# Turning W_v with VectorE and moving a tile's trip ahead of the last loads, in a cross-attention and feed-forward kernel

## The chip, the cores and the metric

The kernel runs on one core of a Trainium2 chip. The metric is the device time of one execution in microseconds (us). TensorE does matrix products and turns (transposes) into PSUM, VectorE and ScalarE do elementwise work, GpSimd a few small steps, and SyncE (SP) issues nearly all transfers from one queue, in order. Each engine runs its instructions in the order of the program and waits on semaphores.

## The reference

```python
x = x + attention(layernorm(x), ctx, Wq, Wk, Wv, Wout, bout)   # 8 heads of 128, 154 keys, softmax
y = layernorm(x)
y_prev = y shifted by one row, zeros in front
xr = mu_r * y + (1 - mu_r) * y_prev;  xk = mu_k * y + (1 - mu_k) * y_prev
r = sigmoid(xr @ W_r.T);  k = relu(xk @ W_k.T) ** 2
out = x + r * (k @ W_v.T)
```

x is (2, 2048, 512), the context (2, 77, 384), W_r, W_k and W_v are (512, 512), all float32. The context rows of both batches serve as 154 keys for every query.

## The kernel before, in words

The 4096 rows of x are 32 tiles of 128 rows. Keys and Wq are folded once into A (512 x 8 heads x 154), values and Wout into B, so a tile needs `scores` (x times A), a softmax over the keys of each head, and `attend` (probabilities times B). The feed-forward part works on pairs of tiles: `gate_rows` (r), `key_columns` (k) and `value_rows`. Every product is done in three passes: both operands are split into a high part, rounded to TensorE's fp32r, and a low part, the rest; high parts are written by ScalarE (`..._hi`), low parts by VectorE (`..._lo`).

Rows have to be turned before a product. The first two tiles of x are turned by TensorE. All others, the probabilities and the second norm's rows make a trip: the rows are stored to DRAM (`store_x`, `store_probs`, `store_x2`), fetched back in four quarters of 32 partitions (`hand_x`, `hand_probs`, `hand_x2`), and VectorE turns the 32 x 32 blocks (`x_turn`, `probs_turn`, `x2_turn`). W_k and W_r are loaded by quarters too (`load_quarters`) and turned by VectorE, four instructions each (`weights_turn`). W_v is loaded by plain rows (`load_rows`) and turned by TensorE in `turn_weights`, 16 turns into four PSUM banks (`W_BANKS`), from where ScalarE takes half of it as the high part and VectorE the low part.

The order of the work is written out by hand for each engine. Ahead of the loop over groups of four tiles (`turns(engine, step)`) stands a prologue that sets up A and B (`values_out`, `values_hi`, `values_lo`, `pack_values`) and works the first tiles in between. In that prologue:

- SyncE issues the loads, the fourth tile's x, `x_early[0]` (the fifth tile), W_v, eight small loads of mu, `x_early[1]`, and then the bias and the third tile's trip (`store_x(2)`, `hand_x(2)`).
- TensorE does the first and second tile's scores, `values_out` block by block (block 4 waits for the low part of block 0, for its bank), scores(2), attend(0), the turns of W_v, scores(3), attend(1), and then the loop, which starts with scores(4), attend(2).
- scores(t) waits for the tile's turned rows (`xT_ready`) and for the exponentials of the tile before, which read the same banks; scores(2) waits for all nine `B_lo`.
- `x_statistics(t)` on VectorE gives mean and variance, `x_root(t)` on GpSimd the factor and shift (three small instructions), `x_norm(t)` on ScalarE the normed rows.

The lines that order VectorE in the stretch that the change touches:

```python
            x_turn(2)
            maxima(1, 2)
            x_statistics(4, None, 1)
            for c in range(6):
                values_lo(c)
            x_lo(2)
            for c in range(6, FULL):
                values_lo(c)
            pack_values()
            probs_turn(0)
```

Of the kernel before, what the change touches and what calls it, by code (L numbers as in the profile page):

```python
# [11 lines left out]
P = 128  # L12
Q = 32
# [6 lines left out]
def xattn_ffn(nc, x, ctx_768, Wq, Wk, Wv, Wout, bout, W_r, W_k, W_v, mu_r, mu_k, out):  # L20
# [18 lines left out]
    HJ = HEADS * J  # L39

# [32 lines left out]
    with ExitStack() as stack:  # L73
# [51 lines left out]
        for w in "kr":  # L125
# [41 lines left out]
                 "v": sb("raw_wv", [P, DC, D], at=at_act)}  # L167
# [65 lines left out]
        Wv_turned, Wv_hi_ready, Wv_ready = sem("Wv_turned"), sem("Wv_hi_ready"), sem("Wv_ready")  # L233
# [91 lines left out]
        W_BANKS = [T[2], XB, T[0], T[1]]  # L325
# [5 lines left out]
        def _(sp):  # L331
# [18 lines left out]
            load_x_in(2)  # L350
            def load_quarters(w, src):
# [7 lines left out]
            sp.dma_start(x_early[0][:], xt[4 * P:5 * P, :]).then_inc(early_loaded[0], 16)  # L359
            load_rows(raw_w["v"], W_v, ffn_loaded["v"])  # L360
            with nc.allow_non_contiguous_dma(reason="two vectors of 512 as columns"):
                for w, src in (("k", mu_k), ("r", mu_r)):
                    for q in range(4):
                        part = src[q * P:(q + 1) * P].rearrange("(k i) -> i k", i=Q)
                        sp.dma_start(mu[w][q * Q:(q + 1) * Q, :], part).then_inc(mu_loaded, 16)  # L365

            sp.dma_start(x_early[1][:], xt[5 * P:6 * P, :]).then_inc(early_loaded[1], 16)

# [73 lines left out]
            def step(g, s):  # L442
# [21 lines left out]
            hand_x(2)  # L464
            sp.wait_ge(consts_ready, 1)
# [28 lines left out]
        def _(te):  # L494
# [64 lines left out]
            def gate_rows(q, j):  # L559
# [46 lines left out]

            def turn_weights(w):

                te.wait_ge(ffn_loaded[w], 16)
                te.wait_ge(exp_done, 6)  # L610
                te.wait_ge(B_ready, FULL)
                for c, bank in enumerate(W_BANKS):
                    for m in range(DC):
# [834 lines left out]
```

## Time and profile before

| what | value |
|---|---|
| median of three runs | 747.12 us (746.11 to 747.29) |
| the profiled execution | 747.18 us, span 745.4 us |
| granted TensorE clock | 1.000 |
| busy in the span | TensorE 737.6 us (99%), VectorE 514.5 (69%), ScalarE 426.1 (57%), GpSimd 123.7 (17%) |
| transfers | 106.52 MB, mean 143 GB/s |

Busy times are of one execution. Times in a timeline are us from the start of the span. A row gives the start, the duration, the engine, the line, what is written from what, and in brackets how long the engine was idle ahead of it and what ended that. Instructions that follow each other on one engine overlap a little, so the distance from start to start is shorter than the duration.

### The profile page before, as it was taken

The numbers are of one execution on the slowest core, as the hardware profiler recorded it, in microseconds if no ns is written. First come the engines' busy times: TensorE is split into PE (matmuls) and PEld (weight loads), VectorE is DVE, ScalarE is ACT, GpSimd is POOL, SyncE is SP. The second block draws the span as 40 slices with busy tenths as digits, with TensorE's granted clock in tenths as the row PEclk, the third lists the DMA queues.
The fourth block names the chain that finished last, engine by engine and source line by source line (L and its number), as shares of the span: only waits on it lengthen the run. The fifth ranks groups of instructions, "written<-read, shape, count | busy, mean of one in ns | idle before, by whom it ended". The sixth has DMA issues, their size and how long they took to land.

```text
span 745.4 us, 13579 instructions
## 1 busy us (share of the span) xinstructions
PE 737.6 (99%) x3964; PEld 643.7 (86%) x3964; DVE 514.5 (69%) x1081; ACT 426.1 (57%) x1204; POOL 123.7 (17%) x279
## 2 busy tenths in 40 slices
PE   9999999999999999999999999999999999999998
PEld 8958888898989888898888889888888988888887
DVE  3679797676777776667777666677666667776662
ACT  3559666564647547564655656465565646555332
POOL 1111010212121020212102021211202121120211
PEclk9999999999999999999999999999999999999999
DMA  8973644555444453544435354443535454343301
GB/s 331 264 203 106 188 115 145 148 150 162 141 132 146 137 158 99 176 134 146 139 120 162 95 176 136 150 133 123 159 105 166 140 163 128 113 155 93 110 29 43
DMA packets 85655, 106.52 MB, mean 143 GB/s; under 512 B 9951, under 2 KB 62073, under 8 KB 85627
## 3 DMA queue, kind: packets, MB, share of 16 engines
q1 hardware_dynamic: 85588, 106.15, 46.7%
q8 instruction: 13, 0.21, 0.1%
q14 instruction: 15, 0.12, 0.1%
q10 hardware_dynamic: 39, 0.04, 0.0%
HBM read 58.70 MB, written 47.45 MB: 142 GB/s over the span
## 4 chain that ended last, share of the span: by engine, by line
PE 86%; SPq 5%; DVE 4%; ACT 1%; issue 1%; DMA 1%; POOL 0%; DVEq 0%; POOLq 0%; ACTq 0%
PE ffn L497 12%; PE ffn L499 12%; PE ffn L498 12%; PE scores L498 8%; PE scores L499 8%; PE scores L497 8%; PE attended L498 8%; PE attended L499 8%; PE attended L497 8%; SPq L354 2%; SPq L338 1%; PE attended L547 1%; PE attended L546 1%; PE scores L653 1%; SPq L365 1%
## 5 line engine op out<-in xcount | busy, mean ns | idle before, releaser
L497 PE MATMUL scores<-A_hi,xT_hi 128*128 128x462 f32 x372 | 130.0, 349 | 1.1 <-DVE xT_lo L985 1.1
L498 PE MATMUL scores<-A_lo,xT_hi 128*128 128x462 f32 x372 | 130.3, 350 | 0.0
L499 PE MATMUL scores<-A_hi,xT_lo 128*128 128x462 f32 x372 | 129.9, 349 | 0.0
L499 PE MATMUL attended<-B_hi,pT_lo 128*128 128x512 f32 x288 | 112.4, 390 | 0.0
L498 PE MATMUL attended<-B_lo,pT_hi 128*128 128x512 f32 x288 | 112.3, 390 | 0.0
L497 PE MATMUL attended<-B_hi,pT_hi 128*128 128x512 f32 x288 | 112.1, 389 | 0.2 <-DVE pT_lo L985 0.2
L788 ACT ACTIVATE probs<-scores,neg_max 128x154 f32<-128x154 f32 x248 | 93.2, 388 | 33.2 <-DVE neg_max L1045 32.8
L1045 DVE TENSOR_REDUCE neg_max<-scores 128x3 f32<-128x462 f32 (+1 forms) x93 | 53.1, 583 | 70.8 <-PE scores L499 70.8
L1338 POOL TENSOR_SCALAR var<-stats 128x1 f32<-128x1 f32 x64 | 12.4, 194 | 461.8 <-DVE stats L991 460.8
L497 PEld LDWEIGHTS scores<-A_hi,xT_hi 128*128 128x128 f32 x372 | 70.1, 189 | 8.6 <-DVE xT_lo L985 1.6
L498 PEld LDWEIGHTS scores<-A_lo,xT_hi 128*128 128x128 f32 x372 | 70.0, 188 | 5.6
L499 PEld LDWEIGHTS scores<-A_hi,xT_lo 128*128 128x128 f32 x372 | 69.9, 188 | 5.2
L985 DVE TENSOR_TENSOR pT_lo<-pT,pT_hi 128x512 fp32r<-128x512 f32 (+1 forms) x96 | 47.9, 554 | 38.3 <-ACT pT_hi L814 38.2
L497 PE MATMUL ffn<-xk_hi,WkT_hi 128*128 128x256 f32 x256 | 72.6, 283 | 0.1
L499 PE MATMUL ffn<-xk_hi,WkT_lo 128*128 128x256 f32 x256 | 72.4, 283 | 0.0
L498 PE MATMUL ffn<-xk_lo,WkT_hi 128*128 128x256 f32 x256 | 72.4, 283 | 0.0
L762 ACT ACTIVATE normed<-x_in,shift,rstd 128x512 f32<-128x512 f32 x30 | 24.5, 815 | 71.0 <-POOL shift L1343 70.5
L797 ACT ACTIVATE probs<-probs,inv_sum 128x154 f32<-128x154 f32 x192 | 63.9, 426 | 0.6 <-DVE inv_sum L1056 0.4
L499 PEld LDWEIGHTS attended<-B_hi,pT_lo 128*128 128x128 f32 x288 | 54.1, 188 | 11.3
L497 PEld LDWEIGHTS attended<-B_hi,pT_hi 128*128 128x128 f32 x288 | 54.1, 188 | 10.7 <-issue 0.4
L498 PEld LDWEIGHTS attended<-B_lo,pT_hi 128*128 128x128 f32 x288 | 54.0, 188 | 10.4
L1005 DVE STREAM_TRANSPOSE pT<-probs_handed 128x1408 f32<-128x1408 f32 x32 | 52.6, 1644 | 0.1
(176 smaller groups left out, 1549.2 us busy)
## 6 DMA issues: line engine op xcount, KB each, us to landing
prob_rows<-probs SPq DMA_DIRECT2D x32, 704.0 KB, 3.4
probs_handed<-prob_rows SPq DMA_DIRECT2D x128, 176.0 KB, 3.3
x_rows<-normed SPq DMA_DIRECT2D x61, 256.0 KB, 2.1
handed<-x_rows SPq DMA_DIRECT2D x244, 64.0 KB, 1.9
x_in<-in_x SPq DMA_DIRECT2D x32, 256.0 KB, 3.6
out<-x SPq DMA_DIRECT2D x31, 256.0 KB, 2.3
wq<-in_L_xattn_Wq SPq DMA_DIRECT2D x2, 1024.0 KB, 10.4
wout<-in_L_xattn_Wout SPq DMA_DIRECT2D x1, 2048.0 KB, 19.5
```

Of the source, the lines that this page charges most:

```text
L338: sp.dma_start(x_in[i][:], xt[i * P:(i + 1) * P, :]).then_inc(x_loaded[i], 16)
L354: sp.dma_start(raw_w[w][q * Q:(q + 1) * Q, :, :], rows[q]).then_inc(ffn_loaded[w], 16)
L497: te.matmul(psum, left[0], right[0], start=first, stop=False)
L498: te.matmul(psum, left[0], right[1], start=False, stop=False)
L499: return te.matmul(psum, left[1], right[0], start=False, stop=last)
L762: nc.scalar.activation(to, rows, ACT.Identity, bias=shift1[:], scale=rstd1[:]).then_inc(xn_ready, 1)
L788: last = nc.scalar.activation(probs[:, q, cols], score_banks(t)[b][:, (h - h0) * J:(h - h0 + 1) * J], ACT.Exp, bias=neg_max[:, h:h + 1], a ...
L797: last = nc.scalar.mul(probs[:, q, cols], probs[:, q, cols], inv_sum[:, h:h + 1])
L985: return v.tensor_tensor(dst, value, hi.bitcast(F32), ALU.subtract)
L1005: return v.transpose(dst.rearrange("p k (r i) -> p r k i", i=Q), src.rearrange(blocks, r=4, k=width, i=Q))
L1045: v.tensor_reduce(neg_max[:, h0:h1], score_banks(t)[b][:, 0:(h1 - h0) * J].rearrange("p (h j) -> p h j", j=J), X, ALU.max, negate=True).th ...
L1338: gp.tensor_scalar(var[:], stats[:, 1:2], EPS, 1.0, ALU.add, ALU.mult).then_inc(var_ready, 1)
```

## The change

1. W_v is loaded by quarters like W_k and W_r, and VectorE turns it (four instructions). TensorE's 16 turns are gone, and with them their wait and the banks. ScalarE's high part and VectorE's low part of W_v read the turned copy in SBUF; the copy lies where the low part will be.
2. W_k's turned rows come in another order, which fits the order of the values that the turned W_v expects.
3. SyncE issues the bias and the third tile's trip right behind the fourth tile's load. `x_early[0]`, W_v, the mu loads and `x_early[1]` follow it, ahead of `store_probs(0)`.
4. VectorE does `values_lo` 0 to 3 ahead of `x_turn(2)`; the turns of W_v stand between the last `values_lo` and behind them; `x_statistics(4)` comes behind the low parts of the first probabilities. `weights_lo("v")` comes behind `maxima(3, ...)`, `x_turn(4)` and `x_lo(4)` ahead of other steps, and `add_x(1)` ahead of `pack_lo(3)`.
5. In the loop, `load_x` stands ahead of `store_probs` on SyncE, `x_statistics` ahead of `open_values` on VectorE, and `x_root` ahead of `output` on GpSimd.

```diff
@@ allocations @@
-            if w != "v":
-                turned_w[w] = sb(f"W{w}T", [P, DC, D], at=at_low)
+            turned_w[w] = sb(f"W{w}T", [P, DC, D], at=at_low)
...
-                 "v": sb("raw_wv", [P, DC, D], at=at_act)}
+                 "v": sb("raw_wv", [P, 4 * DC, P], at=at_act)}
@@ sync @@
             load_quarters("r", W_r)
             load_x_in(3)
-            sp.dma_start(x_early[0][:], xt[4 * P:5 * P, :]).then_inc(early_loaded[0], 16)
-            load_rows(raw_w["v"], W_v, ffn_loaded["v"])
-            ...
-            sp.dma_start(x_early[1][:], xt[5 * P:6 * P, :]).then_inc(early_loaded[1], 16)
...
+                if is_tile(t + 4) and is_tile(t):
+                    load_x(t + 4, s)
                 if is_tile(t + 2):
                     store_probs(t + 2)
-                if is_tile(t + 4) and is_tile(t):
-                    load_x(t + 4, s)
...
             load_bias()
             store_x(2)
             hand_x(2)
+            sp.dma_start(x_early[0][:], xt[4 * P:5 * P, :]).then_inc(early_loaded[0], 16)
+            load_quarters("v", W_v)
+            ...
+            sp.dma_start(x_early[1][:], xt[5 * P:6 * P, :]).then_inc(early_loaded[1], 16)
             sp.wait_ge(consts_ready, 1)
             store_probs(0)
@@ tensor @@
-                    te.wait_ge(W_ready, 2 * DC)
-                    te.wait_ge(Wv_ready, DC)
+                    te.wait_ge(W_ready, 3 * DC)
...
             attend(0)
-            turn_weights("v")
             scores(3)
@@ scalar @@
             def weights_hi(w):
                 for c in range(DC):
+                    act_e.wait_ge(W_turned, DC * "krv".index(w) + DC)
                     if w == "v":
-                        act_e.wait_ge(Wv_turned, c + 1)
-                        nc.scalar.mul(WT[w][0][:, c, :], W_BANKS[c][:], 0.5).then_inc(Wv_hi_ready, 1)
+                        nc.scalar.mul(WT[w][0][:, c, :], turned_w[w][:, c, :], 0.5).then_inc(W_hi_ready, 1)
@@ vector @@
                 dve.wait_ge(ffn_loaded[w], 64)
-                to = turned_w[w][:].rearrange("p k (b r i) -> p b r k i", r=4, i=Q)
+                if w == "v":
+                    dve.wait_ge(W_turned, 2 * DC)
+                order = "p k (r b i) -> p b r k i" if w == "k" else "p k (b r i) -> p b r k i"
+                to = turned_w[w][:].rearrange(order, r=4, i=Q)
...
+                if comes_in_steps(t + 3):
+                    x_statistics(t + 3, (s + 3) % 4, g + (s + 3) // 4 + 1)
                 if half == 0 and is_pair(q - 1) and not is_last(t - 1):
                     open_values(q - 1, 1)
-                if comes_in_steps(t + 3):
-                    x_statistics(t + 3, (s + 3) % 4, g + (s + 3) // 4 + 1)
...
             maxima(1, 1)
+            maxima(1, 2)
+            for c in range(4):
+                values_lo(c)
             x_turn(2)
-            maxima(1, 2)
-            x_statistics(4, None, 1)
-            for c in range(6):
+            for c in range(4, 6):
                 values_lo(c)
             x_lo(2)
+            weights_turn("v", range(0, 1))
             for c in range(6, FULL):
                 values_lo(c)
+                weights_turn("v", range(c - 5, c - 4))
             pack_values()
...
             for i in range(3):
                 probs_lo(0, i)
+            x_statistics(4, None, 1)
...
-            weights_lo("v")
             for b in range(3):
                 maxima(3, b)
+            weights_lo("v")
+            x_turn(4)
             inverse_early(3)
-            x_turn(4)
+            x_lo(4)
             normalise_late(3)
-            x_lo(4)
+            add_x(1, 0, 1)
             pack_lo(3)
-            add_x(1, 0, 1)
@@ gpsimd @@
+                if comes_in_steps(t + 3):
+                    x_root(t + 3)
                 if half == 0 and is_pair(q - 1):
                     output(q - 1, 1, (s + 1) % 4)
-                if comes_in_steps(t + 3):
-                    x_root(t + 3)
```

## Rows read from the trace of the kernel before

**Rows 1.** Windows view, 180 to 700 us: busy us of each engine, granted clock.

```profile
180.00:700.00 520.00, 520.00 (x2714) 457.06 (x2713) 361.99 (x770) 300.18 (x863) 90.53 (x192) 1.00 0.45 139
```

**Rows 2.** Timeline of TensorE, prologue: start, us, line, what, idle before.

```profile
48.13 1.04 PE L653 MATMUL spare<-wout,vT 128*32 128x512 f32 x8
50.45 1.06 PE L653 MATMUL scores<-wout,picked 128*32 128x512 f32 x8 [1.28 <-DVE B_lo L985]
...
57.46 0.48 PE L497 MATMUL scores<-A_hi,xT_hi 128*128 128x462 f32 x1
...
70.88 0.60 PE L614 MATMUL ffn<-identity,raw_wv 128*128 128x128 f32 x4
...
72.55 0.46 PE L497 MATMUL scores<-A_hi,xT_hi 128*128 128x462 f32 x1
...
79.36 0.39 PE L497 MATMUL attended<-B_hi,pT_hi 128*128 128x512 f32 x1
...
87.27 0.48 PE L497 MATMUL scores<-A_hi,xT_hi 128*128 128x462 f32 x1 [1.15 <-DVE xT_lo L985]
```

**Rows 3.** Waits of TensorE: who for whom, us in total, times, longest.

```profile
PE attended L497 <- DVE pT_lo L985: 0.2, 1, 0.2
```

**Rows 4.** Timeline of VectorE, prologue.

```profile
39.11 0.69 DVE L988 BATCH_NORM_STATS2 raw<-x_in 128x6 f32<-128x512 f32 x1 [1.26 <-DMA x_in<-in_x]
...
44.42 1.30 DVE L1145 STREAM_TRANSPOSE WrT<-raw_wr 128x512 f32<-128x512 f32 x2
...
47.86 0.72 DVE L1005 STREAM_TRANSPOSE xT<-handed 128x512 f32<-128x512 f32 x1 [1.63 <-DMA handed<-x_rows]
...
49.64 0.18 DVE L991 BATCH_NORM_AGGREGATE stats<-raw 128x2 f32<-128x6 f32 x1
...
53.92 0.69 DVE L985 TENSOR_TENSOR B_lo<-scores,B_hi 128x512 fp32r<-128x512 f32 x1 [0.17 <-ACT B_hi L860]
...
56.50 0.69 DVE L985 TENSOR_TENSOR B_lo<-scores,B_hi 128x512 fp32r<-128x512 f32 x1
57.66 0.69 DVE L1166 TENSOR_TENSOR packed_rows<-scores,bias_rows 128x512 f32<-128x512 f32 x1 [0.48 <-PE scores L653]
...
62.56 1.49 DVE L985 TENSOR_TENSOR pT_lo<-pT,pT_hi 128x512 fp32r<-128x512 f32 x3
...
78.11 1.50 DVE L985 TENSOR_TENSOR pT_lo<-pT,pT_hi 128x512 fp32r<-128x512 f32 x3 [0.69 <-ACT pT_hi L814]
...
81.95 1.56 DVE L1045 TENSOR_REDUCE neg_max<-scores 128x3 f32<-128x462 f32 x3
...
86.52 0.69 DVE L985 TENSOR_TENSOR xT_lo<-xT,xT_hi 128x512 fp32r<-128x512 f32 x1
```

**Rows 5.** Timeline of ScalarE, prologue.

```profile
64.56 0.81 ACT L762 ACTIVATE normed<-x_early,shift,rstd 128x512 f32<-128x512 f32 x1
...
71.06 0.38 ACT L788 ACTIVATE probs<-scores,neg_max 128x154 f32<-128x154 f32 x1
```

**Rows 6.** Timeline of GpSimd: last of x_root's three instructions, fifth and sixth tile.

```profile
51.01 0.27 POOL L1343 TENSOR_SCALAR shift<-stats,rstd 128x1 f32<-128x1 f32 x1 [0.18 <-POOL rstd L1340]
...
67.75 1.28 POOL L1343 TENSOR_SCALAR shift<-stats,rstd 128x1 f32<-128x1 f32 x1 [0.18 <-POOL rstd L1340]
```

**Rows 7.** Timeline of SyncE's queue: start and duration of the issues.

```profile
16.46 7.38 SPq L354 DMA_DIRECT2D raw_wk<-in_L_ffn_W_k  x4
...
33.33 3.50 SPq L365 DMA_DIRECT2D mu_k_cols<-in_L_ffn_mu_k  x4
...
46.43 0.36 SPq L397 DMA_DIRECT2D prob_rows<-probs  x1
...
49.61 1.91 SPq L406 DMA_DIRECT2D probs_handed<-prob_rows  x4
```

**Rows 8.** DMA view, 24 to 30 us, while W_k and W_r load.

```profile
DMA packets 2130, 1.18 MB, mean 197 GB/s; under 512 B 73, under 2 KB 2047, under 8 KB 2130
```

**Rows 9.** Tile probs_handed, 49 to 60 us.

```profile
DMA to landing us min/median/max: 2.7/3.5/4.4
```

More of the change, by code:

```diff
@@ L358, in _ @@
             load_x_in(3)
-            sp.dma_start(x_early[0][:], xt[4 * P:5 * P, :]).then_inc(early_loaded[0], 16)
-            load_rows(raw_w["v"], W_v, ffn_loaded["v"])
[L361 to L365, printed above, removed]
-            sp.dma_start(x_early[1][:], xt[5 * P:6 * P, :]).then_inc(early_loaded[1], 16)
             def load_bias():
@@ L464, in _ @@
             hand_x(2)
+            sp.dma_start(x_early[0][:], xt[4 * P:5 * P, :]).then_inc(early_loaded[0], 16)
+            load_quarters("v", W_v)
+            with nc.allow_non_contiguous_dma(reason="two vectors of 512 as columns"):
+                for w, src in (("k", mu_k), ("r", mu_r)):
+                    for q in range(4):
+                        part = src[q * P:(q + 1) * P].rearrange("(k i) -> i k", i=Q)
+                        sp.dma_start(mu[w][q * Q:(q + 1) * Q, :], part).then_inc(mu_loaded, 16)
+            sp.dma_start(x_early[1][:], xt[5 * P:6 * P, :]).then_inc(early_loaded[1], 16)
             sp.wait_ge(consts_ready, 1)
@@ L605, in last_value_rows @@
                     last.then_inc(last_done, 1)
[L607 to L613, printed above, removed]
-                        last = te.transpose(bank[:, m * P:(m + 1) * P], raw_w[w][:, m, c * P:(c + 1) * P], identity[:])
-                    last.then_inc(Wv_turned, 1)
             def step(g, s):
@@ L848, in weights_hi @@
                 for c in range(DC):
+                    act_e.wait_ge(W_turned, DC * "krv".index(w) + DC)
                     if w == "v":
-                        act_e.wait_ge(Wv_turned, c + 1)
-                        nc.scalar.mul(WT[w][0][:, c, :], W_BANKS[c][:], 0.5).then_inc(Wv_hi_ready, 1)
+                        nc.scalar.mul(WT[w][0][:, c, :], turned_w[w][:, c, :], 0.5).then_inc(W_hi_ready, 1)
                     else:
-                        act_e.wait_ge(W_turned, DC * "kr".index(w) + DC)
                         copy(WT[w][0][:, c, :], turned_w[w][:, c, :]).then_inc(W_hi_ready, 1)
@@ L1149, in weights_lo @@
                     hi, lo = WT[w][0][:, c, :], WT[w][1][:, c, :]
+                    dve.wait_ge(W_hi_ready, DC * "krv".index(w) + c + 1)
                     if w == "v":
-                        dve.wait_ge(Wv_hi_ready, c + 1)
-                        v.scalar_tensor_tensor(out=lo, in0=W_BANKS[c][:], scalar=0.5, in1=hi.bitcast(F32),
-                                               op0=ALU.mult, op1=ALU.subtract).then_inc(Wv_ready, 1)
+                        v.scalar_tensor_tensor(out=lo, in0=turned_w[w][:, c, :], scalar=0.5, in1=hi.bitcast(F32),
+                                               op0=ALU.mult, op1=ALU.subtract).then_inc(W_ready, 1)
                     else:
-                        dve.wait_ge(W_hi_ready, DC * "kr".index(w) + c + 1)
                         low_part(lo, turned_w[w][:, c, :], hi).then_inc(W_ready, 1)
```

2 lines of the change are left out of this document (removed).

## Prediction

> **What bounds the kernel now.** I read the busy times by stretch first: from 180 to 700 us TensorE computes 520.00 of 520 us, with VectorE and ScalarE well below [rows 1]; what little it idles lies ahead of 100 us or at the very end. So only three things can move the end: TensorE work taken away or added, gaps closed or opened in the prologue, and a stage that becomes slower than TensorE. The edits inside the loop cannot pay: there is no gap there to close. The list of waits of TensorE and its timeline then give what the prologue has to give: one gap in front of the fifth values block, where block 3 starts at 48.13 and block 4 at 50.45. Block 4 (twice the work) to block 10 take from 50.45 to the scores at 57.46, so a single one about 0.86, and block 4 could start at 48.99: 1.46 us. The turns of W_v run from 70.88 to 72.55: 1.67 us of work. The last gap is in front of the fifth tile's scores: they start at 87.27, while attention that starts at 79.36 and lasts 6.60 ends at 85.96: 1.31 us [rows 2]. A small one of 0.2 us follows ahead of the third tile's attention [rows 3]. All together 4.6 us, 0.6% of the time: that is the most the change can bring.
>
> **The removed gap at the values.** It was made by VectorE: it waited 1.63 us for the third tile's trip, turned it at 47.86, and only behind that came the first B_lo (statistics of the fifth tile, whose second half is at 49.64, stood between too) [rows 4]. The new order does B_lo 0 to 3 first, and the trip's turn behind them, so block 4 starts at 48.99. From there the B_hi parts come 1.46 us earlier. But VectorE now has other work in that stretch: one turn of W_v ahead of each of B_lo 6, 7, 8, at 0.61 us from start to start (two in a row took 1.30 with their overlap, the row at 44.42). B_lo 5 starts at 53.92 - 1.46 = 52.46; x_lo 53.06; turn 53.66; B_lo 6 54.27; turn 54.87; B_lo 7 55.48; turn 56.09; B_lo 8 at 56.70, against 56.50 before [rows 4]. The third tile's scores wait for all nine: 56.70 + 0.69 = 57.39, against a start at 57.46 [rows 2]. **Term 1: 0.0 us.** The gap of 1.46 moves from block 4 to just ahead of these scores. The fourth turn stands ahead of pack_values: 57.91 instead of 57.66, and so does all that VectorE does behind it: +0.25.
>
> **The removed turns on TensorE.** The fourth tile's scores could start at 70.9 instead of 72.55. They need bank 0 free, that is the third exponential of the third tile: the fourth one starts at 71.06 [rows 5], so 71.1 is the floor even with nothing late. But ScalarE will be late. Its queue has the fifth tile's x_norm ahead of W_k's and W_r's high parts and of those exponentials. It ran at 64.56 without a wait, because the statistics were from 49.64 [rows 4, 5]. Now x_statistics(4) stands behind the low parts of the first tile's probabilities. These start at 62.56 + 0.25 = 62.81 and take 1.41; the statistics start at 64.22, the aggregate at 65.02. From aggregate to x_norm there are GpSimd's three instructions: aggregate at 49.64, third one from 51.01 to 51.28, so 1.64 and a hop of 0.04: x_norm at 66.70, **2.14 us late** [rows 4, 6]. The other bound of that trip: the same third instruction took 1.28 instead of 0.27 when it ran beside W_k's low parts (67.75) [rows 6], so up to 1.0 more; I take the short one, since maxima (which read one operand in PSUM) will run beside it. ScalarE has no slack to lose in this stretch: the casts, the exponentials and the normalisation follow back to back. So bank 0 comes free at 71.1 + 2.14 = 73.3 and the scores start there, 0.8 later than before, though TensorE was ready at 70.9.
>
> The same 2.14 travel on: normalise, pack_hi, pack_lo, the turn of the second tile's probabilities, and their first low part at 78.11 + 2.14 = 80.25 [rows 4], complete at 80.8. Scores end at 73.4 + 6.8 = 80.2, so attention starts at 80.85 against 79.36 [rows 2] and ends at 87.5. From 80.25 VectorE does what stood from 78.11 to 81.95 (three low parts of the probabilities and four of W_v, 3.84), three maxima (1.56, less the overlap 1.46) and the turn of the fifth tile (0.64 to the next start) [rows 4]: 86.2; ScalarE's exponentials of the fourth tile end at 86.3 and its x_hi at 86.9; x_lo ends at 87.6. Before, x_lo started at 86.52 and ended at 87.2 [rows 4]. Here the lateness is mostly absorbed, for the old order had ScalarE wait for the maxima behind W_v. **Term 2: the fifth tile's scores start at 87.7 instead of 87.27: +0.43.** The 1.67 us of turns have become waiting for ScalarE.
>
> **The moved loads.** SyncE's queue is in order. The third tile's store and trip come ahead of x_early, W_v, eight mu parts and x_early. The last tile load ahead of it lands at 39.1 (VectorE waits for it until 39.11 [rows 4]); the store lands right behind, about 40.1. Then four issues of the trip 1.9, x_early 0.4, W_v's four, the mu parts, x_early 0.4, and only then store_probs(0), which was issued at 46.43 [rows 7]. Four issues cost 1.9 with an empty queue (49.61) and 7.4 behind a full one (16.46). The queue is empty here: I take 1.9. Four mu parts took 3.50, so eight 3.8 to 7.0; I take 5.4 [rows 7]. That gives 50.1 for store_probs(0), 3.7 late. It landed 3.2 after its issue (46.43 to 49.61). W_v now comes in pieces of 512 bytes like W_r: 2130 packets in 6 us [rows 8], so 2048 take 5.8 us, from 42.5 to 48.3, and the mu parts are behind them: I put the landing at 54.0 against 49.6. Trip issued over 1.9, landing 2.7 to 4.4 behind the last issue [rows 9]: complete 58.2 to 59.9, I take 59.4. VectorE wants it at 57.91 + 0.80 = 58.71. **Term 3: 0.7 us** (0 to 1.2 by these rows). It moves the whole chain of term 2 one for one. By a fit of the Trainium skill (DMA: Bandwidth & Descriptors, Anatomy of one DMA, made for GpSimd's path) a transfer takes about 2.0 us and its bytes at 436 GB/s, whatever the size of its pieces; that would be an estimated 4.4 us for W_v's megabyte, it would be through before the mu parts are issued, and the sum would be 747.2. The row, 197 GB/s with pieces of 512 bytes, speaks against it [rows 8]. W_v itself is needed at 53.66 and landed about 50, so its new wait costs nothing; were it late, B_lo 6 to 8 and the third tile's scores stand behind it.
>
> **What costs nothing.** W_v's low parts now read SBUF instead of PSUM: the tensor_tensor of both kinds goes at 0.60 from start to start. W_k's turned row order changes an output stride only. add_x(1) ahead of pack_lo(3) starts 1 us earlier the trip to the second tile's x2_norm, on which the third attention waited: the 0.2 gap and its restart (0.3) go: **term 4: -0.3**. In the loop, statistics ahead of open_values, load_x ahead of store_probs and x_root ahead of output move waits of engines that TensorE does not wait for [rows 1]. If that cover were gone, load_x would cost store_probs about 0.9 us (wait for x2 and an issue) per tile.
>
> **Sum.** 0.0 + 0.43 + 0.7 - 0.3 = +0.8 us on a span of 745.4, whose execution took 747.18; the median of the runs is 747.12. Forecast 747.9.
>
> **The rivals.**
> A, faster: ScalarE's lateness doesn't arise, because x_statistics(4) or its GpSimd trip finds a place earlier, or ScalarE's chain has slack that the rows don't show. Then only the +0.25 of VectorE's queue is left. Scores at 71.4, attention at 79.0 (its low parts at 78.36 + 0.55), x_lo(4): 78.36 + 3.84 + 1.46 + 0.64 = 84.3, ScalarE's x_hi and x_lo 1.3: 85.6. That is 1.6 earlier, and with term 4 745.2. With no chain of VectorE in the way the limit is 747.1 - 4.6 = 742.5. For it: TensorE really loses 1.67 us of work. Against: [rows 5, 6], in which nothing hides the trip through GpSimd.
> B, slower: the probabilities' trip is what decides. W_v's issues go at the speed of W_k's: 7.4 instead of 1.9, and store_probs(0) follows at 55.6, it is through at 58.8, and the trip lands about 63.8, 5.1 behind 58.71: 752.3. It decides from the point where the trip lands over 60.1 (1.4 behind 58.71), which is +1.5. For it: these are the same strided quarters. Against: W_k was issued behind all the attention's weights, W_v behind nothing. In between lies 749 to 750, with a loaded queue or the slow GpSimd trip (+1.0).
> C: the probabilities arrive in time; term 3 is 0, 747.2. It is also what the Trainium skill's fit above would give.
>
> **How the numbers follow.** Forecast 0.42 (747.2 to 748.6), C 0.16, A 0.15, B and what lies between 0.27. A measurement of this kernel tells about 0.2%, 1.5 us, from no change. C and the forecast are within it: same 0.58; A faster 0.15; B slower 0.27. The likeliest case's own range is 747.0 to 748.7; with A's first figure and the lower half of B the range is 745.2 to 750.0.
>
> **What the profile after would show.** TensorE's waits: none ahead of block 4, a new one of 1 to 1.5 us ahead of the third tile's scores at 57.4 (from B_lo), one of about 2 ahead of the fourth tile's (from the exponentials, near 73), a short one at 80, and the fifth tile's scores at 87.7 or later. ScalarE: an idle of about 2 us ahead of x_norm(4), ended by GpSimd's shift. VectorE: a wait for the probabilities at 58.7 that is term 3. The prediction is wrong if x_norm(4) runs near 65, or if store_probs(0) is issued near 48 or near 55.

## The result, and the profile after

| | kernel before | kernel after |
|---|---|---|
| median, 19 runs each | 747.21 us (745.94 to 749.98) | 747.90 us (746.79 to 749.16) |
| ratio to before | | 1.0013 [1.0007, 1.0019] |
| profiled execution | 747.18 us, span 745.4 | 747.85 us, span 746.1 |

The time went up by 0.13%, which is inside the 0.2% that the prediction held for "no change". A later comparison of the kernel before with itself gave 1.0011 [1.0002, 1.0020], so a tenth of a per cent is at the limit of what can be told here. The forecast was 747.9. As will be seen, part of that agreement is luck: the sum held one term that didn't arise, and lacked two effects that did.

The busy times on the page after (busy us, share of the span, instructions):

```profile
PE 737.1 (99%) x3948; PEld 644.1 (86%) x3948; DVE 516.5 (69%) x1085; ACT 428.2 (57%) x1204; POOL 123.6 (17%) x279
```

The longest of TensorE's waits after (us in total, times, longest):

```profile
PE scores L494 <- ACT probs L773: 2.3, 1, 2.3
PE scores L494 <- DVE B_lo L969: 1.4, 1, 1.4
PE ffn L650 <- DVE normed L1208: 1.0, 1, 1.0
PE attended L494 <- DVE pT_lo L969: 0.4, 1, 0.4
```

The window of [rows 1] in the kernel after:

```profile
180.00:700.00 520.00, 520.00 (x2714) 457.11 (x2714) 361.77 (x771) 300.81 (x859) 88.89 (x188) 1.00 0.45 139
```

The loop is as full as before. (The 1.0 on `normed` is in the first two us of the span, in both kernels.) Two waits stand in the prologue where there were none: 1.4 us for the last B_lo and 2.3 us for the exponentials. This is where they are in TensorE's timeline, with the start of the first tile's scores ahead of them:

```profile
33.34 0.45 PE L494 MATMUL scores<-A_hi,xT_hi 128*128 128x462 f32 x1
...
58.89 0.45 PE L494 MATMUL scores<-A_hi,xT_hi 128*128 128x462 f32 x1 [1.41 <-DVE B_lo L969]
...
74.75 0.45 PE L494 MATMUL scores<-A_hi,xT_hi 128*128 128x462 f32 x1 [2.29 <-ACT probs L773]
...
82.15 0.47 PE L494 MATMUL attended<-B_hi,pT_hi 128*128 128x512 f32 x1 [0.41 <-DVE pT_lo L969]
```

And the same start before:

```profile
31.92 0.45 PE L497 MATMUL scores<-A_hi,xT_hi 128*128 128x462 f32 x1
```

Here is the first thing to see. Ahead of these scores both programs issue the same matmuls, and yet one profile comes to them at 31.92 and the other at 33.34. Over all 14 profiles of this study it is 31.3 to 33.8. (What sets it is told in the last section.) So a profile after can't be laid on one of before by the clock on the wall. From here on TensorE's steps are counted from the start of the first scores, and "less 1.42" turns a time of the profile after into one of before. The steps, from the timelines (us from the first scores; the last column is from the first key_columns to the end of the span):

| kernel | first scores at | third tile's scores | fourth's | second attention | fifth's scores | third attention | key_columns | to the end | from first scores to the end |
|---|---|---|---|---|---|---|---|---|---|
| before | 31.92 | 25.54 | 40.63 | 47.44 | 55.35 | 62.48 | 71.88 | 641.60 | 713.48 |
| before, again | 32.51 | 25.32 | 40.42 | 47.24 | 55.13 | 62.27 | 71.69 | 641.40 | 713.09 |
| after | 33.34 | 25.55 | 41.41 | 48.81 | 55.46 | 62.23 | 71.54 | 641.22 | 712.76 |
| after, again | 33.41 | 25.55 | 41.41 | 48.80 | 55.51 | 62.27 | 71.58 | 641.21 | 712.79 |

Read by row, the change is 0.8 to 1.0 late at the fourth tile's scores, 0.1 to 0.4 late at the fifth's, level or up to 0.3 ahead at the third attention, and from the first key_columns to the end it takes 0.2 to 0.4 less. From the first scores to the end it is 0.3 to 0.7 us **shorter** than before, though its time is 0.7 longer. That is what the experiments have to explain, besides the two waits.

The instructions on which terms 2 and 3 rested, VectorE first:

```profile
55.09 0.70 DVE L1132 STREAM_TRANSPOSE WvT<-raw_wv 128x512 f32<-128x512 f32 x1
...
58.09 0.65 DVE L969 TENSOR_TENSOR B_lo<-scores,B_hi 128x512 fp32r<-128x512 f32 x1
58.67 0.69 DVE L1132 STREAM_TRANSPOSE WvT<-raw_wv 128x512 f32<-128x512 f32 x1
...
60.04 1.65 DVE L989 STREAM_TRANSPOSE pT<-probs_handed 128x1408 f32<-128x1408 f32 x1
...
66.34 0.18 DVE L975 BATCH_NORM_AGGREGATE stats<-raw 128x2 f32<-128x6 f32 x1
...
81.31 1.50 DVE L969 TENSOR_TENSOR pT_lo<-pT,pT_hi 128x512 fp32r<-128x512 f32 x3 [0.69 <-ACT pT_hi L799]
```

GpSimd's last step for the fifth tile's x_norm:

```profile
67.70 0.27 POOL L1333 TENSOR_SCALAR shift<-stats,rstd 128x1 f32<-128x1 f32 x1 [0.18 <-POOL rstd L1330]
```

and the x_norm itself on ScalarE:

```profile
68.00 0.82 ACT L747 ACTIVATE normed<-x_early,shift,rstd 128x512 f32<-128x512 f32 x1 [1.76 <-POOL shift L1333]
```

SyncE's queue (start and duration of the issues):

```profile
40.86 2.47 SPq L353 DMA_DIRECT2D raw_wv<-in_L_ffn_W_v  x4
43.37 2.67 SPq L460 DMA_DIRECT2D mu_k_cols<-in_L_ffn_mu_k  x4
46.08 1.86 SPq L460 DMA_DIRECT2D mu_r_cols<-in_L_ffn_mu_r  x4
47.99 0.43 SPq L461 DMA_DIRECT2D x_early<-in_x  x1
48.53 0.36 SPq L386 DMA_DIRECT2D prob_rows<-probs  x1
...
52.68 2.40 SPq L395 DMA_DIRECT2D probs_handed<-prob_rows  x4
```

No idle time stands in front of the turns of W_v or of the turn of the probabilities: both had landed. ScalarE waited 1.76 us for GpSimd's shift, as a chain of one statistics, one trip through GpSimd and one x_norm.

### The profile page after: what moved, and what is told of

Read it like the earlier page. It is cut to its first block, busy times and chain, and to the rows that moved or that the text cites. A ratio compares the mean times of both kernels' runs of the same rounds, so it can differ in the third digit from the quotient of the medians.

```text
span 746.1 us, 13557 instructions
## 1 busy us (share of the span) xinstructions
PE 737.1 (99%) x3948; PEld 644.1 (86%) x3948; DVE 516.5 (69%) x1085; ACT 428.2 (57%) x1204; POOL 123.6 (17%) x279
## 3 DMA queue, kind: packets, MB, share of 16 engines
HBM read 58.70 MB, written 47.45 MB: 142 GB/s over the span
## 4 chain that ended last, share of the span: by engine, by line
PE 93%; DVE 3%; ACT 2%; issue 1%; POOL 0%; POOLq 0%; DVEq 0%; ACTq 0%
PE ffn L494 12%; PE ffn L496 12%; PE ffn L495 12%; PE scores L495 9%; PE scores L496 9%; PE scores L494 9%; PE attended L496 8%; PE attended L495 8%; PE attended L494 8%; PE attended L544 1%; PE attended L543 1%; PE scores L670 1%; PE scores L639 1%; PE scores L701 1%; PE ffn L701 1%
## 5 line engine op out<-in xcount | busy, mean ns | idle before, releaser
L830 ACT ACTIVATE gate<-ffn 128x512 f32<-128x512 f32 x32 | 19.2, 598 | 64.0 <-PE ffn L496 64.0
```

The costliest lines, as they stand in the source:

```text
L830: nc.scalar.activation(gate[half][:], T[0][:], ACT.Tanh, scale=0.5).then_inc(gate_ready, 1)
```

## The experiments

The theory to be tested was the prediction's: the turns' time on TensorE has become two waits, one for VectorE's B_lo and one for ScalarE behind a late x_norm, and the probabilities' trip decides a further 0.7. Its rivals were those of the prediction: that ScalarE's lateness costs nothing (A's side), and that the moved loads and the trip behind them decide (B's side). All ratios are to the kernel before, run beside each.

**after_again.** The changed kernel, unchanged, beside the first three edits.

> The changed kernel once more, unchanged. In the profiles so far TensorE's first scores start at 31.92 us (before) and 33.34 us (after), though nothing ahead of them is changed, while from there to the end the changed kernel is 0.7 us shorter. If that head is chance, it will differ from run to run and the first scores start anywhere from 31.9 to 33.5 or later; from them to the end the profile again takes 712.8 us. If the head belongs to the changed program, the first scores start at 33.3 again. Ratio to the kernel before: 1.000 to 1.002.

Measured: 749.0 us, ratio 1.0026 [1.0015, 1.0037], 8 runs; 712.79 from the first scores. All steps fall on those of the first profile to 0.05 us. The median is 1.1 above that of the first comparison, though the work is the same: see the clock, below.

**stats_early.** The fifth tile's statistics back to where they had been relative to the maxima; all else as after.

```diff
             maxima(1, 2)
+            x_statistics(4, None, 1)
             for c in range(4):
...
                 probs_lo(0, i)
-            x_statistics(4, None, 1)
```

> The changed kernel with the fifth tile's statistics in VectorE's idle time ahead of the first B_lo, where its load has landed. Theory (ScalarE waits for x_norm(4) and hands the wait on to the fourth tile's scores): no wait of ScalarE ahead of x_norm(4), the wait of TensorE for the exponentials ahead of the fourth tile's scores falls from 2.3 to about 0.5 us, from first scores to end 1.8 us shorter than the changed kernel (711.0), ratio to before about 0.9985. Rival (the time is lost to VectorE's added turns and the quartered load of W_v): the wait moves elsewhere and the span stays within 0.4 us of the changed kernel's.

Measured: 746.21 us, 0.9982 [0.9973, 0.9992]; 711.13 from the first scores, 1.6 less than after. TensorE's waits:

```profile
PE scores L494 <- DVE B_lo L969: 1.4, 1, 1.4
...
PE attended L494 <- DVE pT_lo L969: 0.7, 1, 0.7
PE scores L494 <- ACT probs L773: 0.4, 1, 0.4
```

The wait for the exponentials fell from 2.3 to 0.4, and nothing ahead of it moved. So the moved statistics were the cause of it, through GpSimd and ScalarE's queue: term 2's chain is shown.

**turns_late.** W_v's turns out from between the B_lo, one by one into later places; W_r's second low parts make room.

```diff
             x_lo(2)
-            weights_turn("v", range(0, 1))
             for c in range(6, FULL):
                 values_lo(c)
-                weights_turn("v", range(c - 5, c - 4))
...
             add_x(0, 0, 0)
+            weights_turn("v", range(0, 1))
...
-            weights_lo("r", range(2, 4))
+            weights_turn("v", range(1, 3))
             pack_lo(2)
             probs_turn(1)
+            weights_turn("v", range(3, 4))
...
             inverse_early(3)
+            weights_lo("r", range(2, 4))
```

> The changed kernel with W_v's four turns taken from between the last B_lo and put into later idle times of VectorE (two low parts of W_r move behind for them). Theory: the wait of 1.4 us for B_lo ahead of the third tile's scores is gone, they start 25.5 us behind... that is 24.1 us instead of 25.55 us behind the first scores; VectorE and ScalarE are about 2 us earlier from there, x_norm(4) still waits for GpSimd; first scores to end 1.4 to 2.0 us shorter than the changed kernel. Rival: the trip of the first probabilities, now behind W_v's load, lands too late for the earlier turn, VectorE waits for it and less than 0.8 us is won.

Measured: 747.18 us, 1.0004 [0.9993, 1.0015]; 711.95 from the first scores. The third tile's scores came at 24.07 instead of 25.55 and the wait for B_lo was gone, so term 1 is shown: the three turns took up the 1.46 us of the gap that the new order had closed. The fourth tile's scores were still 1.6 earlier than in after (39.79 against 41.41). But only 0.8 of 1.5 was left at the end. TensorE's timeline tells why:

```profile
73.34 0.45 PE L494 MATMUL scores<-A_hi,xT_hi 128*128 128x462 f32 x1 [2.12 <-ACT probs L773]
73.62 0.37 PE L495 MATMUL scores<-A_lo,xT_hi 128*128 128x462 f32 x1
73.83 0.37 PE L496 MATMUL scores<-A_hi,xT_lo 128*128 128x462 f32 x1
...
75.57 0.59 PE L496 MATMUL scores<-A_hi,xT_lo 128*128 128x462 f32 x1
75.95 0.59 PE L494 MATMUL scores<-A_hi,xT_hi 128*128 128x462 f32 x1
...
77.88 0.40 PE L496 MATMUL scores<-A_hi,xT_lo 128*128 128x462 f32 x1
78.12 0.38 PE L494 MATMUL scores<-A_hi,xT_hi 128*128 128x462 f32 x1
```

The windows of the same stretch (busy time and count of TensorE, its weight loads, VectorE, ScalarE, GpSimd, then the granted clock, the DMA share and GB/s):

```profile
73.30:74.40 1.10, 1.06 (x5) 1.02 (x6) 1.00 (x3) 1.10 (x7) 0.17 (x1) 1.00 1.14 224
74.40:77.90 3.50, 3.50 (x12) 3.00 (x11) 2.73 (x8) 3.47 (x13) 0.86 (x3) 0.51 0.27 50
```

The like stretch in the profile of after_again:

```profile
74.80:78.00 3.20, 3.18 (x15) 2.91 (x16) 2.24 (x7) 3.20 (x16) 1.57 (x3) 1.00 0.66 140
```

Behind an idle of 2.12 us TensorE took up work at 0.21 us from start to start, and from 74.45 to 77.88 it went at 0.38: the granted clock of that window is 0.51, the lower level of 1.2 GHz. It did there nine matmuls in the time of some sixteen: about 1.5 us lost, of which 1.0 is seen at the second attention. It came 8.36 behind the fourth tile's scores instead of 7.40 in after, where some 0.6 had gone into waiting anyway (without a wait it is 6.8, as in before). The Trainium skill (TensorE: Matmul & The Clock Gate, Back-to-back issue gap) gives, for a matmul by itself, the columns divided by the clock from start to start, and 2.5 ns more at the upper level. By that 462 columns at 1.2 GHz are an estimated 0.385 us, and the trace agrees (0.384 on the mean of seven); at 2.4 GHz they would be 0.195, where the trace has 0.21. In after_again's profile the clock stayed whole behind the same wait.

**both.** The two edits together.

> Both edits. If the two waits stand in one chain, the gains add: about 3 us from first scores to end against the changed kernel, ratio to before 0.996 to 0.997. If ScalarE, busy without a gap from 60 to 80 us, is the limit, the second edit adds less than half of what it brings alone.

Measured: 745.9 us, 0.9986 [0.9974, 0.9997]; but 712.93 from the first scores, no less than after, where 3 us less was expected. The first scores began at 31.27 in this profile, the earliest of all, and VectorE waited for the probabilities' trip:

```profile
58.70 1.65 DVE L989 STREAM_TRANSPOSE pT<-probs_handed 128x1408 f32<-128x1408 f32 x1 [2.47 <-DMA probs_handed<-prob_rows]
```

TensorE's waits in it:

```profile
PE attended L494 <- DVE pT_lo L969: 2.6, 2, 1.4
PE scores L494 <- ACT probs L773: 1.1, 1, 1.1
```

The trip landed at 58.7 here and by about 58.6 in the profile after, though TensorE began 2 us earlier here. With VectorE's queue 2.4 shorter and TensorE 2 us early, that is late. So in this order the wait of term 3 exists, and it depends on when the first scores begin.

**both_probs_first.** both, with the mu loads and x_early[1] behind the probabilities' trip.

```diff
-            [mu loads, x_early[1]]
             sp.wait_ge(consts_ready, 1)
             store_probs(0)
             store_x(3)
             hand_probs(0)
             hand_x(3)
+            [mu loads, x_early[1]]
```

> The variant with both edits, and SyncE does the whole trip of the first probabilities and of the fourth tile ahead of the mu loads and x_early 1. In the profile with both edits VectorE waited 2.5 us for that trip, which landed at 58.7. Theory: the trip lands before VectorE wants it (about 56), the third tile's attention follows its scores, and from first scores to end the two gains add at last: 709.8 to 710.6 us, ratio to before 0.9955 to 0.997. Rival: ScalarE, which has no idle time from 60 to 80 us, is the limit, and it stays at 711.1 like the early statistics alone.

Measured: 745.52 us, 0.9972 [0.9960, 0.9984]; 710.63 from the first scores, which began at 33.77. hand_probs(0) was issued at 50.27 instead of 53.41, and VectorE turned the probabilities at 58.85 without a wait. A new wait of 1.3 us for pT_lo came ahead of the second attention, where the moved turns of W_v now stand. As the head differed by 2.5 us between this profile and that of both, the 2.3 us between them are not the edit's alone.

**mu_late and stats_early_mu_late.** The same loads behind store_probs(0) and store_x(3) only, in after and in stats_early.

```diff
+            sp.wait_ge(consts_ready, 1)
+            store_probs(0)
+            store_x(3)
             [mu loads, x_early[1]]
-            sp.wait_ge(consts_ready, 1)
-            store_probs(0)
-            store_x(3)
```

> The changed kernel with the eight loads of mu and x_early 1 issued behind the store of the first probabilities and of the fourth tile, in the time in which SyncE waits for the store to land. store_probs(0) is issued 5 us earlier (about 44 instead of 48.5), but its trip waits for the issues of mu, so hand_probs(0) starts at 50 to 51 instead of 52.7. If the moved loads cost the changed kernel time through the first probabilities' trip when TensorE's head is early (term 3 of the prediction), the median falls by 0.3 to 0.9 us. If VectorE's turns alone set the turn of these probabilities, nothing changes: 0.0 +- 0.2.

> The variant with early statistics, and the mu loads late. ScalarE's wait is gone and the trip is earlier: with an early head the whole gain of 1.65 us shows from first scores to end (711.1) and the median is 0.3 to 0.9 us below that of the early statistics alone; if the trip never matters, the same as with early statistics alone, ratio to before 0.998.

Measured: 747.53 us, 1.0006 [0.9997, 1.0015], and 712.76 from the first scores, with the same steps and waits as after to 0.03 us; 745.88 us, 0.9983 [0.9974, 0.9992], and 711.17 against 711.13. In the profiles of after's order the probabilities' trip is not on the path, and term 3 is zero. (No profile of after itself has an early head, so for those executions this rests on the medians, which hardly differ.) The second also repeats stats_early with a head of 31.73 in place of 33.27, and its profiled span is 742.9 against 744.4: in these kernels a late head goes through to the end, one for one.

**old_loads.** After, with x_early[0], W_v's quarters, the mu loads and x_early[1] ahead of the bias and the trip, where the kernel before has them.

> The changed kernel with the loads in their old order: x_early 0, W_v by quarters, mu and x_early 1 ahead of the third tile's trip. It shows what the moved trip is worth once W_v comes in pieces of 512 bytes. The queue is loaded there, so W_v's four issues should take 5 to 7 us and the third tile's store be issued at 44 to 48; its turn on VectorE, now behind four B_lo, waits 1 to 6 us, and the third tile's scores and all behind them are 1 to 5 us late: 714 to 718 us from first scores to end. If the issues go at 0.5 us each, it is within 0.5 us of the changed kernel's 712.8.

Measured: 747.72 us, 1.0008 [0.9999, 1.0018]; 714.45 from the first scores, 1.7 more than after. W_v's four issues took 3.85 us, less than expected. SyncE's queue:

```profile
37.23 4.97 SPq L364 DMA_DIRECT2D mu_k_cols<-in_L_ffn_mu_k  x4
42.25 2.07 SPq L364 DMA_DIRECT2D mu_r_cols<-in_L_ffn_mu_r  x4
...
45.67 0.38 SPq L375 DMA_DIRECT2D x_rows<-normed  x1
...
48.19 1.75 SPq L380 DMA_DIRECT2D handed<-x_rows  x4
```

hand_x(2) goes at 48.19 instead of 38.59, TensorE waits 0.6 us for B_lo at a values block, and the third tile's scores are 0.8 later (26.35). The fourth tile's scores are 0.8 later too (42.22 against 41.41), but the second attention is 1.8 later (50.58 against 48.81). Between them lies a fall of the clock like that of turns_late; its window, from about 1 us behind the wait for the exponentials:

```profile
75.70:79.20 3.50, 3.50 (x11) 3.01 (x10) 2.47 (x7) 3.47 (x13) 1.42 (x3) 0.51 0.29 57
```

So with W_v in quarters the moved trip is worth 0.8 us by the steps, and the other 0.9 of this profile are the clock's. The medians don't show even the 0.8: old_loads is at 1.0008, after at 1.0013 and 1.0026.

**trip_first_only.** The kernel before, with the trip ahead of the loads and VectorE's maxima, statistics and four values_lo ahead of the trip's turn. W_v stays in plain rows on TensorE, the loop stays.

```diff
+            [bias, store_x(2), hand_x(2)]
             [x_early[0], load_rows W_v, mu loads, x_early[1]]
-            [bias, store_x(2), hand_x(2)]
...
-            x_turn(2)
             maxima(1, 2)
             x_statistics(4, None, 1)
-            for c in range(6):
+            for c in range(4):
+                values_lo(c)
+            x_turn(2)
+            for c in range(4, 6):
                 values_lo(c)
```

> The kernel before with only the third tile's trip ahead of the loads, B_lo 0 to 3 ahead of its turn, and the statistics of the fifth tile ahead of those; W_v is loaded by rows and turned by TensorE as before. Theory: the gap of 1.46 us at values block 4 closes and nothing fills it, the third tile's scores start 24.1 us behind the first instead of 25.54, VectorE's chain is earlier by as much, and from first scores to end it takes 1.0 to 1.5 us less than before (712.0 to 712.5), as good as or better than the full change (712.8). Rival: what the full change gains comes from the turns taken off TensorE, then this one gives less than 0.5 us.

Measured: 746.50 us, 0.9990 [0.9981, 0.9999]; 711.92 from the first scores. The third tile's scores came at 24.07: the gap ahead of block 4 was closed with one part of the change, and this part alone ends 0.8 to 0.9 earlier than the whole.

**loop_only.** The kernel before, with the three edits of the loop.

> The kernel before with only the three edits inside the loop (load_x ahead of store_probs, statistics ahead of open_values, x_root ahead of output). The prediction costs them at nothing: the first 100 us are as before, and from the first key_columns to the end it takes 641.2 to 641.6 us as before. If one of them delays a step that TensorE needs, the stretch is longer by 0.1 us or more per tile, 3 us or more.

Measured: 746.50 us, 0.9990 [0.9980, 0.9999]; from the first key_columns to the end 641.25 against 641.60 and 641.40. But it also had no gap ahead of block 4, which lies ahead of the loop and which nothing in it could have closed: the third tile's scores came at 24.08. Its head was 33.80. VectorE's row for the trip's turn:

```profile
47.74 0.71 DVE L1005 STREAM_TRANSPOSE xT<-handed 128x512 f32<-128x512 f32 x1 [0.65 <-DMA handed<-x_rows]
```

TensorE's rows of blocks 3 and 4:

```profile
50.04 1.04 PE L653 MATMUL spare<-wout,vT 128*32 128x512 f32 x8
50.90 1.04 PE L653 MATMUL scores<-wout,picked 128*32 128x512 f32 x8
```

The trip landed at 47.7 as before (47.86 in [rows 4]), but TensorE was 1.9 us later, so there was nothing left to wait for. In the kernel before, then, the gap takes up what the head loses: its profiled spans are 745.4, 745.6 and (with the loop's edits) 745.5 for heads of 31.92, 32.51 and 33.80.

**base_again.** The kernel before, unchanged: see the table above.

> The kernel before once more, unchanged. The profiles of the changed kernel and of two variants had their first scores at 33.3 to 33.6 us, those of the kernel before and of the variant with both edits at 31.9 and 31.3. If the head is chance in every program, this profile may show either, and from first scores to end it takes 713.5 us. If the changed programs have the later head by themselves, this one shows 31.9 or earlier again. Ratio to the kernel before 1.000.

Measured: 747.34 us, 1.0011 [1.0002, 1.0020]; 713.09 from the first scores.

**pe_turns_full.** trip_first_only with the loop's edits and the new order of VectorE at the fourth tile: all of the change but for W_v's turns, which stay on TensorE, and the statistics, which stay ahead of values_lo. It differs from stats_early in who turns W_v, how it is loaded, where its low parts come from, and the order of W_k's turned rows.

```diff
+            [the three edits of the loop]
-            weights_lo("v")
             for b in range(3):
                 maxima(3, b)
+            weights_lo("v")
+            x_turn(4)
             inverse_early(3)
-            x_turn(4)
+            x_lo(4)
             normalise_late(3)
-            x_lo(4)
+            add_x(1, 0, 1)
             pack_lo(3)
-            add_x(1, 0, 1)
```

> The variant with early statistics, all its orders kept, but W_v loaded by rows and turned by TensorE as before. It isolates the turns. If taking 1.67 us of turns off TensorE is worth something by itself, this one is slower than the early statistics (711.1 us from first scores to end), by up to 1.7 us. If VectorE's four added turns give it back, both take the same within 0.3 us, since without them the third tile's scores start 1.46 us earlier.

Measured: **743.58 us, 0.9952 [0.9939, 0.9966]**, the fastest of the study, 3.6 us below the kernel before, in five runs. From the first scores to the end it took 709.82, 1.3 less than stats_early. (The two ratios, 0.9952 and 0.9982, lie some 2.2 us apart; the steps account for 1.3 of it. The rest may be the heads of the runs, which only a profile shows.) All of TensorE's waits:

```profile
PE ffn L663 <- DVE normed L1221: 1.0, 1, 1.0
PE scores L592 <- ACT normed L771: 0.3, 1, 0.3
PE ffn L697 <- DMA wq<-in_L_xattn_Wq: 0.3, 1, 0.3
```

All three lie ahead of the first scores or at the end of the span. Its turns of W_v, with the fourth tile's scores right behind:

```profile
69.50 0.60 PE L613 MATMUL ffn<-identity,raw_wv 128*128 128x128 f32 x4
69.93 0.60 PE L613 MATMUL spare<-identity,raw_wv 128*128 128x128 f32 x4
70.37 1.04 PE L613 MATMUL ffn<-identity,raw_wv 128*128 128x128 f32 x8
71.16 0.46 PE L496 MATMUL scores<-A_hi,xT_hi 128*128 128x462 f32 x1
```

The 1.66 us of turns are paid, and the view shows no wait of TensorE between the first scores and 718 us.

## Why the prediction came out as it did

**What bounds the kernel.** Right. The loop is full in every profile, and all that moved lay in the prologue, but for 0.2 to 0.4 us. Of the 4.6 us that the gaps and turns had to give, pe_turns_full took 3.3 to 3.7 (709.82 against 713.09 and 713.48): the gaps, without the turns, and the loop's part.

**Term 1, 0.0.** Right, to 0.01 us: 25.55 against 25.54, and the gap of 1.41 in front of these scores instead of block 4. B_lo 8 at 58.09 less 1.42 is 56.67; forecast 56.70. turns_late shows that the three turns are the cause.

**Term 2, +0.43.** The mechanism is right, step by step: x_norm(4) at 66.58 (forecast 66.70), the fourth tile's scores at 73.33 (73.4), the second attention at 80.73 (80.85), all less 1.42. The short value for GpSimd's third instruction was the right one (0.27). The size at the fifth tile's scores was off: 0.11 instead of 0.43 (0.3 against the kernel before's second profile). The step that failed there is "the same 2.14 travel on ... their first low part at 78.11 + 2.14 = 80.25": it came at 81.31 less 1.42, 79.89, and the 0.36 are what is missing at the end. x_norm itself was 2.02 late, and 0.24 more were made up on ScalarE, where the normalisation starts right behind the last exponential; in the kernel before it started 0.27 later than that. stats_early shows the cause of the lateness and what it is worth: 1.65.

**Term 3, +0.7.** This failed: it was 0. The prediction named store_probs(0) near 48 as a sign against it, and it was issued at 48.53, not 50.1. The step that failed first is the start of the third tile's trip. The prediction let its store land at 40.1, behind the last tile load of the queue; hand_x(2), which waits for that store, was issued at 38.59, and this 1.5 is nearly all of the 1.6. Behind it W_v's issues took 2.47 (1.9 taken) and the mu loads 4.53 (5.4 taken), together 0.3 less. The store of the probabilities was through by 52.68 at the latest (54.0 taken), and the pieces of the trip landed 2.6 to 3.5 us behind their issues, so by about 58.6 (59.4 taken); both shows 58.70. VectorE wanted them at 60.04. Less 1.42 that is 58.62, near the forecast's 58.71. So with a head as early as before's the two would just have met: the measured 0 is the lower of the term's bounds (0 to 1.2). The sum set a landing that goes by the wall's clock against a wish that moves with TensorE's head. mu_late settles that nothing hangs on it at a head of 32.94; for the earliest heads it stays open whether a few tenths do. The Trainium skill's fit (DMA: Bandwidth & Descriptors, Anatomy of one DMA), which made this rival C, doesn't hold for W_v: for a quarter of 262144 bytes it gives an estimated 2.6 us, and the rows have 4.7 to 6.7 from issue to landing. The trip was in time without it.

**Term 4, -0.3.** Right: from the fifth tile's scores to the third attention 6.77 instead of 7.13, and no wait there.

**The loop, 0.** A little off: from the first key_columns to the end the eleven profiles with the loop's edits take 641.2 to 641.3, the three without 641.4 to 641.6. That is 0.1 to 0.4 us less; the medians can't tell it from nothing, and what brings it was not looked for.

**What the sum left out.** By its steps the change should have ended 0.3 to 0.7 earlier, and its time was 0.7 later. Two effects lie between. Each is shown in profiles; how much each weighs in the medians is argued, since a run without a profile doesn't show its head:

- **The head.** In the kernel before the gap ahead of block 4 is a wait for a trip that lands near 47.8 on the wall's clock, so it absorbs a late head (loop_only). The new order ends that dependence, and then a late head costs all that it is late: 745.7, 746.1 and 746.2 for heads of 32.94, 33.34 and 33.41 (mu_late and the two of after). The prediction took a gap of 1.46 as something that can be won; in executions with a late head it isn't there.
- **The clock.** 12 of the 19 runs of after had a mean granted clock of 1.000 and a median of 747.74 us; the other 7 had 0.998 or 0.995, and a median of 749.06. That is 1.3 us more; turns_late's profile shows 1.5 of TensorE's time lost in one stretch behind the wait, 1.0 of it at the next step. Over the kernels whose longest wait in the prologue is 2.1 to 2.3 us (after, after_again, mu_late, old_loads, turns_late) 29 of 60 runs were at 0.998 or below. Over stats_early, stats_early_mu_late, trip_first_only, both_probs_first, loop_only and pe_turns_full, where it is 1.4 or less, none of 56 was; nor was any of the 87 runs of the kernel before beside them. It isn't the wait alone: mu_late had 1 of 11 with the same wait, and base_again 1 of 11 and both 2 of 12 without it. Two profiles have the fall, turns_late and old_loads, both about 1 us behind that wait. That it is at the same place in after's own runs is argued, since both profiles of after have the clock whole. Its price in the medians isn't settled either: between the runs with and without the lower mean clock it is 0.7 in turns_late (10 and 2 runs) and 0.1 in old_loads (5 and 5), where the head, unknown in them, may hide it.

So the wait of term 2 was priced at its length; in a part of the executions a fall of the clock comes with it, and in the two profiles that have it that cost about 1.0 more at the next step.

**The rivals.** A, the faster one, needed the statistics at an earlier place; stats_early is just that, at 746.2 (A said 745.2). B did not arise: W_v's issues went at 2.47, near the lower bound. C is what the trace shows (the trip in time); its 747.2 lacked the two effects above, as the forecast did. That the forecast's 747.9 fell on the median is in part luck: errors of opposite sign.

**Where the gain of the turns went.** 1.67 us of work left the engine that bounds the kernel, and 2.4 us came onto VectorE, just where VectorE's chain sets when scores(2) may start. pe_turns_full against stats_early says it in one number: by the steps, leaving the turns on TensorE is 1.3 us better. In both_probs_first, where the turns stood later, the chain of the second tile's probabilities took their place as the limit. TensorE came to the fourth tile's scores 1.26 earlier than in pe_turns_full (37.92 against 39.18), and yet the second attention started 0.2 later (46.17 against 46.00), behind a wait of 1.3. VectorE's first low part for it began at 45.33 there and at 44.74 in pe_turns_full. Attention started 0.84 behind that in both_probs_first, so an estimate from these rows is that with no turn at all in VectorE's way it could start at 45.6, 0.4 earlier than with the turns on TensorE. By that estimate most of the 1.67 us of turns lay in time that TensorE would have waited. It isn't settled whether a place for them exists where they would cost nothing.

## What to carry to other kernels

Work taken off the engine that is busy 99% of the time pays only if the engine that receives it is not the one whose chain decides when the next step may start: look for the gap that the moved work will open, and undo the parts one at a time. Here the new orders alone are worth 3.6 us by the medians (3.3 to 3.7 by the steps), and the turned W_v with the late statistics took them back. When a gap is a wait for a transfer, ask whether the transfer is fixed in time while the waiting engine moves; such a gap shrinks by itself when the engine is late, and what it seems to offer depends on the execution. And where a change opens a wait of TensorE of some 2 us, look at the granted clock behind it in more than one profile: here two of five such profiles paid for it again.

## What the runs showed of the hardware that was not expected

- In turns_late TensorE, after 2.12 us of idle, first ran on at full speed (matmuls 0.21 us apart, to 74.45) and only then, with no idle at all, at the lower level (0.38 us apart to 77.88, granted clock 0.51). The Trainium skill (TensorE: Matmul & The Clock Gate, A second HAM failure mode: psum-queue depth-cycling) tells of short idle stretches that come often between groups of matmuls and make the clock go back and forth; here it was a single idle and a single fall, which is near that case and not the same. old_loads has the same picture: idle of 2.3 us, scores from 74.67, the lower level from 75.7 to 79.1. In the profiles of after the same idle of 2.29 us left the clock whole.
- The first scores start anywhere from 31.3 to 33.8 us though the same work is ahead of them. In the profile after TensorE did 5 or 6 matmuls per us from 5 to 9 us and then 9 or 10; in the one of before it was at 8 to 10 from 5 us on, but for a short idle. The view says a granted clock of 1.00 for both, but that is no reading: the clock's record in the trace begins only where the pace changes, at 4.6 us in the profile before and at 9.2 in the one after. Over the 14 profiles it begins between 4.3 and 10.2: at 4.4 and 10.1 with W_v turned by VectorE (both, both_probs_first), at 4.3 and 10.2 with TensorE's turns (trip_first_only, loop_only), and in two executions of the kernel before at 4.6 and 7.5. The first scores follow it. In the nine profiles where it begins at 7.4 us or later each us more puts them 0.5 us back (32.45 at 7.45 in old_loads, 33.80 at 10.15 in loop_only); where it begins earlier they start at 31.3 to 32.0. So the head's spread goes with the moment at which TensorE's clock comes up, and that varies from one execution to the next of the same kernel. Two windows of the kernel after:

```profile
5.00:6.00 1.00, 1.00 (x5) 1.00 (x6) 0.00 (x0) 0.47 (x1) 0.00 (x0) 1.00 0.86 320
...
9.00:10.00 1.00, 1.00 (x9) 1.00 (x8) 0.00 (x0) 0.00 (x0) 0.00 (x0) 1.00 1.04 401
```

and the first of them in the kernel before:

```profile
5.00:6.00 1.00, 1.00 (x8) 0.82 (x8) 0.00 (x0) 0.37 (x1) 0.00 (x0) 1.00 0.98 229
```
